# Cross-attention and experts on one core: maxima further ahead, the chain behind the row sums spread over three pairs, fewer projections among the first maxima, and the experts' high halves on ScalarE

## What is computed

```python
def xattn(x, context, Wq, Wk, Wv, Wo, bo):      # x 4x256x128 (normalized), context 4x1601x96
    q, k, v = heads(x @ Wq), heads(context @ Wk), heads(context @ Wv)
    attn = softmax(q @ k.T * 64 ** -0.5)
    return merge(attn @ v) @ Wo + bo
def ffn(h, router_w, router_b, sw1, sb1, sw2, sb2, rw1, rb1, rw2, rb2):   # 1024 tokens
    p = softmax(h @ router_w + router_b)
    weights = p where p is among the top 2 of its row, else 0
    shared = gelu(h @ sw1 + sb1) @ sw2 + sb2
    routed = sum_e weights[:, e] * (gelu(h @ rw1[e] + rb1[e]) @ rw2[e] + rb2[e])
    return shared + routed
x = x + xattn(layernorm(x), ctx)
x = x + ffn(layernorm(x))
```

## Time and profile before

| | us |
|---|---|
| median of 3 runs (lowest to highest) | 484.85 (482.22 to 485.1) |
| the profiled execution | 482.24 |
| its span, first to last instruction | 480.4 |
| PE busy / DVE / ACT / POOL in the span | 453.5 / 288.0 / 185.3 / 310.0 |
| mean share of TensorE's clock that was granted | 0.964 |

### The profile page before, as it was taken

One profiled execution on the slowest core, in us unless ns is written; L12 is line 12 of the kernel. 1 busy time (PEld: TensorE's weight loads), 2 busy tenths in 40 slices (PEclk: granted clock), 3 DMA queues, 4 the chain that ended last, 5 costly groups with the idle time before them and its releaser, 6 DMA issues.

```text
span 480.4 us, 7162 instructions
## 1 busy us (share of the span) xinstructions
PE 453.5 (94%) x2541; PEld 341.6 (71%) x2541; DVE 288.0 (60%) x569; ACT 185.3 (39%) x257; POOL 310.0 (65%) x203
## 2 busy tenths in 40 slices
PE   6989989999999899999999799999998999998896
PEld 5876757776777577767777577768776766676785
DVE  4587865665246646753466665644464437997675
ACT  4443422343544323435434232345341445454341
POOL 5939792876356937673659376745474586677682
PEclk9799998999999979999999799999997999999999
DMA  8200010000000100000002100000000000000000
GB/s 244 80 1 1 0 53 0 2 1 0 1 0 2 53 0 1 0 1 1 1 1 57 43 1 1 0 1 2 0 1 1 1 0 1 1 0 1 23 3 22
DMA packets 5194, 7.27 MB, mean 15 GB/s; under 512 B 644, under 2 KB 4136, under 8 KB 5160
## 3 DMA queue, kind: packets, MB, share of 16 engines
q1 hardware_dynamic: 5160, 6.81, 4.9%
HBM read 6.29 MB, written 0.52 MB: 14 GB/s over the span
## 4 chain that ended last, share of the span: by engine, by line
PE 86%; DVE 11%; issue 1%; ACT 1%; DVEq 0%; POOL 0%; ACTq 0%; POOLq 0%
PE ps L1076 20%; PE ps L1059 11%; PE ps L986 11%; PE ps L1060 10%; PE ps L1061 10%; PE ps L915 6%; PE ps L917 6%; PE ps L916 6%; DVE ps L807 3%; PE ps L1004 1%; PE ps L998 1%; DVE g_hi L891 1%; PE ps L992 1%; DVE probs L874 1%; DVE maxes L794 1%
## 5 line engine op out<-in xcount | busy, mean ns | idle before, releaser
L687 ACT ACTIVATE probs<-ps 128x1024 f32<-128x1024 f32 (+1 forms) x112 | 107.9, 963 | 169.0 <-PE ps L1061 167.5
L477 POOL TENSOR_TENSOR work<-work,probs 128x1024 f32<-128x1024 f32 x60 | 142.9, 2382 | 42.3 <-ACT probs L687 39.8
L794 DVE TENSOR_REDUCE maxes<-ps 128x1 f32<-128x402 f32 x256 | 135.6, 570 | 53.3 <-PE ps L986 52.5
L1076 PE MATMUL ps<-probs,v_sb 128*64 128x256 f32 (+1 forms) x832 | 96.9, 383 | 0.0
L1059 PE MATMUL ps<-g_hi,ctxT_hi 97*128 97x512 f32 (+1 forms) x208 | 86.6, 416 | 8.5 <-DVE g_hi L802 8.5
L986 PE MATMUL ps<-ctxT_hi,g_hi 96*128 96x402 f32 x256 | 82.6, 386 | 2.4 <-DVE work L810 1.1
L1060 PE MATMUL ps<-g_lo,ctxT_hi 96*128 96x512 f32 (+1 forms) x208 | 84.6, 407 | 0.0
L1061 PE MATMUL ps<-g_hi,ctxT_lo 96*128 96x512 f32 (+1 forms) x208 | 84.2, 405 | 0.0
L1076 PEld LDWEIGHTS ps<-probs,v_sb 128*64 128x64 f32 (+1 forms) x832 | 56.9, 137 | 35.8 <-issue 9.3
L475 POOL TENSOR_TENSOR work<-probs 128x1024 f32<-128x1024 f32 x15 | 35.5, 2367 | 56.8 <-issue 55.1
L986 PEld LDWEIGHTS ps<-ctxT_hi,g_hi 96*128 96x128 f32 x256 | 50.0, 203 | 22.3 <-issue 6.9
(11 more groups left out here) (137 smaller groups left out, 560.0 us busy)
## 6 DMA issues: line engine op xcount, KB each, us to landing
raw<-in_ctx_T_dram SPq DMA_DIRECT2D x3, 600.4 KB, 4.5
work<-in_L_ffn_rw_dram SPq DMA_DIRECT2D x1, 1024.0 KB, 7.4
raw<-in_ctx_T_dram SPq DMA_DIRECT2D x3, 150.8 KB, 2.5
x_sb<-in_x_dram SPq DMA_DIRECT2D x1, 384.0 KB, 5.6
early<-in_WqkT_dram SPq DMA_DIRECT2D x1, 336.0 KB, 4.9
wo_sb<-in_L_xattn_Wo_dram SPq DMA_DIRECT2D x1, 256.0 KB, 5.6
out_dram<-x_sb SPq DMA_DIRECT2D x1, 256.0 KB, 2.2
out_dram<-x_sb SPq DMA_DIRECT2D x2, 128.0 KB, 1.7
```

The source lines that it names most:

```text
L477: ops.tensor_tensor(acc, acc, pr, ALU.add).then_inc(summed, 1)
L687: nc.scalar.activation(probs[0:rows, n % SLOTS, 0:wide, :], s, ACT.Exp, scale=SCALE).then_inc(probs_ready, 1)
L794: v.tensor_reduce(maxes[:, p % 2, i * T + t, blk:blk + 1], src[:, 0:BW], AX.X, ALU.max).then_inc(ring_taken, 1)
L1076: ins = mm(o_bank[DH * i:DH * (i + 1), :], v_sb[0:rows, c, h * DH:(h + 1) * DH], probs[0:rows, n % SLOTS, j, i * S:(i + 1) * S], start=(c ...
```

## The change

It does five things. LEAD goes from 1.5 to 2.5 pairs, with the split of the next batch's context (`ctx`) moved from pair 1 to pair 0, so that maxima of the next batch can follow (`split` in `plan`). The chain behind the row sums is spread: `norm` moves from unit 2 to unit 5 of the second pair after, `xt`, `router`, `exp`, `rank` and `best` from the second to the third pair after, `wrow` to the fourth. At the start only every second maximum of (0,0) is followed by a v0, v0 uses 2 banks in place of 4, shift(0,0) comes before the last four v0 and g(0,1) behind them, the second product of the weights comes later, and 7 + 6 small matmuls whose result nobody reads stand behind the first transposes and behind g(0,0) (REST_1, REST_2). In the experts, ScalarE makes the high halves, and does so one turn later: `split` of a turn follows the Gelus and `weigh` of the next; `hid_w` has 8 slots in place of 4; `spread` follows `first`, and its ring slot is free as soon as `weigh` is done (the small memset `freed` goes). `sums` of (3,3) comes ahead of the first `split`, `exp` directly behind `router`, and `rank`, `best` of the second half ahead of the `split` and `second` of turn 7.

```diff
+REST_1 = 7
+REST_2 = 6
-LEAD = 1.5
+LEAD = 2.5
...
-            put.update({4: ("stats", 1), 8: ("stats", 2), 12: ("normal", 1)})
+            put.update({3: ("stats", 1), 6: ("stats", 2), 9: ("stats", 3)})
...
-            if n == 0 and m >= 3 and n_v0 < chunks:
+            if n == 0 and m >= 3 and m % 2:
...
-            tasks.insert(4, ("m", 1))
+            tasks.insert(8, ("m", 1))
             rest = [("v0", c) for c in range(n_v0, chunks)]
-            tasks += rest[:2] + [("shift", b, p)] + rest[2:]
+            tasks += rest[:2] + [("shift", b, p)] + rest[2:] + [("g",) + order[1]]
...
-              (2, 2): [("norm",)], (4, 2): [("ring", ("xt",))], (5, 2): [("ring", ("router",)), ("exp",)],
-              (6, 2): [("rank",), ("best",)], (3, 3): [("ring", ("wrow",))]}
+              (5, 2): [("norm",)], (2, 3): [("ring", ("xt",))], (3, 3): [("ring", ("router",)), ("exp",)],
+              (4, 3): [("rank",), ("best",)], (1, 4): [("ring", ("wrow",))]}
...
-            if p == 1 and b + 1 < batches and u < blocks:
-                main.append(("ctx", (b + 1, u)))
+            if p == 0 and b + 1 < batches and 0 < u <= blocks:
+                main.append(("ctx", (b + 1, u - 1)))
...
-                if done >= need and (at > pe or pair > n):
+                if done >= need and (at > pe or pair > n or task[0] == "max" and task[1] not in split):
...
-    amid = {2: [("ring", ("y", b))], 5: [("ring", ("xt", b))], 6: [("ring", ("router", last))]}
-    behind = {0: [("ring", ("sums",) + last_pair)], 2: [("ring", ("yt", b))], 3: [("norm", b)],
-              6: [("exp", last)], 7: [("rank", last), ("best", last)]}
+    amid = {0: [("ring", ("sums",) + last_pair)], 2: [("ring", ("y", b))], 5: [("ring", ("xt", b))],
+            6: [("ring", ("router", last)), ("exp", last)], 7: [("rank", last), ("best", last)]}
+    behind = {2: [("ring", ("yt", b))], 3: [("norm", b)]}
...
+            new = list(range(n, n + chunks))
+            out += [("first", i) for i in new]
             if e < experts:
                 out.append(("ring", ("spread", h, e)))
...
-            out += [("split", i) for i in new]
-            if h == 1 and turn == 0:
-                out.append(("ring", ("wrow", last)))
+            out += [("split", i) for i in weighted]
+            weighted = new
...
                     act.wait_ge(v0_filled, w + 1)
-                    nc.scalar.copy(v_sb[0:rows, w, :], ps[0:rows, w % 4, :]).then_inc(v0_taken, 1)
+                    nc.scalar.copy(v_sb[0:rows, w, :], ps[0:rows, w % 2, :]).then_inc(v0_taken, 1)
...
+                elif kind == "split":
...
+                    nc.scalar.copy(hid_hi[:, n % SPLITS, :], activations(n)).then_inc(hid_hi_ready, 1)
...
-                    v.tensor_copy(hid_hi[:, n % SPLITS, :], activations(n)).then_inc(hid_hi_ready, 1)
...
+                    if w == ("g", 0, 0):
+                        for _ in range(REST_2):
+                            mm(ps[0:DH, 7, 0:DH], ones[:], ones[:], start=True, stop=True)
```

More of the change, by code:

```diff
@@ L107, in plan @@
                 main += [("w2", e) for e in range(experts) if e * n_units // experts == u]
-            for ago in (1, 2, 3):
+            for ago in (1, 2, 3, 4):
                 if n < ago:
@@ L133, in plan @@
     index = {w: n for n, w in enumerate(order)}
+    split = {0}
     def ready(task):
@@ L185, in plan @@
             put(x)
+            if kind == "ctx" and w[1] == blocks - 1:
+                split.add(w[0])
         last = kind
@@ L219, in plan_experts @@
                 out += [("second", (i, part)) for i in waiting.pop(0) for part in parts[i // per]]
+            if h == 1 and turn == 0:
+                out.append(("ring", ("wrow", last)))
             if h and turn == LAG - 1:
@@ L265, in build @@
     sorts = [[w for w in ring_list if w[0] == name] for name in ("v", "back")]
-    sorts.append([w for w in ring_list if w[0] not in ("v", "back")])
+    sorts.append([w for w in ring_list if w[0] not in ("v", "back", "spread")])
     nth = {w: k for some in sorts for k, w in enumerate(some)}
@@ L433, in taken @@
                 return out_ready, nth[w] + 1
+            if w[0] == "spread":
+                return hidw_ready, weighed[items.index((w[1], w[2], HK - 1))]
             return ring_taken, nth[w] + 1
         def activations(n):
-            return (hid if items[n][1] == E else hid_w)[:, n % 4, :]
+            return hid[:, n % 4, :] if items[n][1] == E else hid_w[:, n % 8, :]
         def m_parts(i):
@@ L647, in _ @@
                 high_part(0, i)
-            act.wait_ge(s_wv, 16)
-            nc.scalar.copy(wv_hi[:], wv_sb).then_inc(wv_hi_ready, 1)
+                if i == 1:
+                    act.wait_ge(s_wv, 16)
+                    nc.scalar.copy(wv_hi[:], wv_sb).then_inc(wv_hi_ready, 1)
             for kind, w in steps:
@@ L700, in _ @@
                     ins.then_inc(lexp_ready, 1)
+                elif kind == "split":
+                    n = w
+                    if n == 0:
+                        act.wait_ge(scores_ready, LAST_UNIT)
+                    if n >= SPLITS:
+                        act.wait_ge(w2_done, n - SPLITS + 1)
+                    if items[n][1] == E:
+                        act.wait_ge(hid_ready, n + 1)
+                    else:
+                        act.wait_ge(hidw_ready, weighed[n])
+                    nc.scalar.copy(hid_hi[:, n % SPLITS, :], activations(n)).then_inc(hid_hi_ready, 1)
                 elif kind == "first":
@@ L917, in three, with keep_awake @@
                 return mm(dst, a_lo, b_hi, start=False, stop=stop)
+            def keep_awake(n):
+                for _ in range(n):
+                    mm(ps[0:DH, 4, 0:DH], ones[:], ones[:], start=True, stop=True)
             pe.wait_ge(pool_done, 1)
-            for _ in range(WARM):
-                mm(ps[0:DH, 4, 0:DH], ones[:], ones[:], start=True, stop=True)
+            keep_awake(WARM)
             def product_of_weights(i):
```

45 lines of the change are left out of this document (16 added, 29 removed).

## The result

The changed kernel takes 468.36 us (median of 4 runs, 467.81 to 470.0), the kernel before 483.63 beside it: ratio 0.969, 95% interval 0.964 to 0.974. It is faster. The profiled execution is the slowest of the four, 470.0 us, with a span of 468.2 and a granted clock of 0.984 (the other three: 0.988 to 0.991). A ratio counts only runs within 1.5% of the same kernel's quickest, and the kernel before scatters over 475.7 to 485.2 us, so further down I compare the kernels' own medians.

What follows compares the result with a forecast made beforehand. TensorE's order was taken to set the end, so gains come from its waits or clock. 482.24 - 3.8 (start) - 16.1 (shifts) + 0.6 (slots) + 3.7 (experts) = 466.6, called 467 us; range 460 to 477, own range 463 to 471.

Steps and rivals of the forecast that it cites:

- Three shifts: In (1,1), (2,1), (3,1): waits for the shift's copy go, 7.2 us, and half-clock stretches, 8.9; together 16.1 us saved.
- clock falls not tied to the waits: Rival, 17%: the three half-clock stretches come from small transposes and sums and stay; 8.9 us remain, 475.5.
- The `ctx` splits that move ... stand on engines with that same room: nothing: Context splits moved to a batch's first pair: claimed to cost nothing, since their engines have room.
- Slots: Maxima crowding into (0,2), 27 in place of 21: +0.6 us charged for waits for slots.
- The start: Up to the first scores: 29.51 becomes 25.7, 3.8 us saved, assuming the small matmuls keep the clock up.
- Experts, +3.7: Experts' part: high halves on ScalarE a turn later and weights earlier, in sum 3.7 us lost, bounds 0 and +7.
- turns 6 to 12: Experts: low halves of items 12, 13 wait behind rank and best; pause of about 4 us, +1.7 for half clock.
- steady turns: Experts: the longer chain through ScalarE's copies and the low halves adds 0.15 us a turn, +0.5 over the last turns.
- the end: Experts' end: VectorE's last two low halves stand behind GpSimd's of item 33, 7.1 us in place of 5.4, +1.7.
- the rival of slow copies: Rival, 4%: ScalarE's copies in the experts take 1.7 us each while GpSimd works, giving 494 us.
- Experts cost nothing: Rival, 15%: TensorE finds its operands in time, with no pause long enough for the clock: 463 us.
- The lead doesn't help: Rival, 9%: VectorE lags behind the plan, slots block TensorE elsewhere, half of 16.1 and 3.8 is lost: 477 us.

Runs made afterwards that it cites:

- fill_waits: Kernel before, with small matmuls in TensorE's three waits for the shift, ahead of the scores of (1,2), (2,2), (3,2): 476.69 us, ratio 0.990.
- ctx_back: Changed kernel with the ctx splits of batch 1 back in (0,1), where they stood before: 466.69 us, ratio 0.976.
- best_late: Changed kernel with rank and best of the last two batches behind the splits of turn 7 instead of ahead of them: 467.58 us, ratio 0.978.
- both_no_rest: both_moves without the 13 small matmuls of the start: 465.19 us, ratio 0.962.
- norm_early: Changed kernel with stats of batches 1 to 3 behind the start's last projection and their normal products earlier in (0,1): 471.8 us, ratio 0.986.
- all_moves: sums_late with VectorE making the low halves of the last four items instead of the last two: 458.36 us, ratio 0.948.
- both_moves: Changed kernel with batch 1's ctx splits back in (0,1) and the last batches' rank and best behind turn 7's splits: 462.26 us, ratio 0.960.
- sums_late: both_moves with the row sums of (0,0) behind the first scores of (0,2) instead of ahead of its shift: 459.42 us, ratio 0.950.

## Why the prediction was right, and where its terms were not

The time (467 against 468.4) lies in the forecast's own range of 463 to 471. But it is partly luck: two terms were off by 3.5 us and more, in opposite directions. The profiled execution, to which the terms were added up (466.6), took 470.0.

- **Three shifts, -16.1: right.** Counted from the starts of the matmuls, what the pairs (1,1), (1,2), (2,1), (2,2), (3,1) and (3,2) lose against full pace fell from 22.9 to 6.7 us, -16.2. The rival "clock falls not tied to the waits" is out for these three: the stretches went with the waits, and in fill_waits with the idle time alone.
- **"The `ctx` splits that move ... stand on engines with that same room: nothing": the step that failed.** Measured: +3.6 in (0,1), of which ctx_back gives back 3.1. Of these, 2.5 are the splits' own: best_late, with the splits as in the changed kernel but no half-clock stretch there, takes 26.89 for (0,1), ctx_back 24.38. (0,2) lost another 1.1, as its stretch was 6.83 instead of 3.41; that this comes from the splits is not shown, since best_late has them and no stretch there. I looked at who waits for GpSimd's results; what counted was who waits for its ports. The rule on shared ports (the Trainium skill, page "SBUF — State Buffer") I used only to clear ScalarE's copies, and not on the `normal` products. The change had moved these too, in a line that the diff above does not show: before, the three pairs started at 38.87, 51.03 and 56.10 and took 0.93, 0.59 and 0.59; after, at 45.62, 50.91 and 54.67, beside GpSimd's longer queue. In (1,0) and (2,0), which now hold the splits for batches 2 and 3, a projection of `v` waits for ScalarE's copy, 0.4 us each.
- **Slots, +0.6: too small.** (0,2), (0,3), (1,0) and (2,0) lose some 2 us more than before, besides the clock.
- **The start, -3.8: right in kind.** From the first maximum to the first scores before takes 20.95 and after 17.61, against the 17.1 that I summed; the clock stayed up, for which the small matmuls are the likely reason (both_no_rest). First maximum and first scores in the timeline of after, as the earlier trace rows:

```profile
9.56 1.65 PE L1000 MATMUL ps<-ctxT_hi,g_hi 96*128 96x402 f32 x4
...
27.17 0.40 PE L1077 MATMUL ps<-g_hi,ctxT_hi 97*128 97x512 f32 x1
```

  The remaining 1.0 us was lost ahead of the first maximum (9.56 instead of 8.56): the small matmuls of the warm-up (44 records) took 4.96 us instead of 4.08; the same code took 4.28 in best_late.
- **Experts, +3.7: mis-sized, measured +0.2.** Worked out from the Gelus' starts: until turn 6 -1.3 (I had -0.5); turns 6 to 12 -0.2 (I had +2.0 without that 0.5), because the stretch at half clock after the idle time (426.25) took the place of the one at 430.5 and did not come on top of it; steady turns +0.3 (+0.5); the end +1.4 (+1.7). ScalarE's copies took 0.615 us in the mean of 36 and 0.626 at most, so the rival of slow copies is out. The copies by form, first ScalarE's after, then VectorE's before: busy us, mean ns, idle ahead.

```profile
L722 ACT CAST g_hi<-probs 128x512 fp32r<-128x512 f32 x36 | 20.2, 615 | 0.0
L891 DVE CAST g_hi<-probs 128x512 fp32r<-128x512 f32 x36 | 18.6, 556 | 2.0 <-ACT probs L715 1.8
```

The 0.38 us that I took for VectorE's copy is the pace of undisturbed ones. The 36 took 0.556 in the mean, up to 1.57, so a copy on ScalarE costs 0.06 us more and not 0.24. The rule of the Trainium skill, page "Perfetto Trace Analysis", section "Optimizing Scalar/DVE Operations", would have cost up to 8.6 us by my 0.24; by the means it is 2.1. The steady turns and the end, where these copies stand in the chain, cost 1.7 together, and other stages gave it back.

"Experts cost nothing" thus had the price right, but not the reason: there was a wait of 2.80 us and a half-clock stretch behind it, and the terms cancelled. "The lead doesn't help" was wrong.

## What to carry to other kernels

Before moving work onto an engine with room, look not only at who waits for its results but at what another engine does in the gaps that the move closes: here 3.5 us of low parts in GpSimd's gaps held up VectorE's products and made (0,1) 2.5 to 3.1 us longer. When a wait ends in a half-clock stretch, the two are two gains: a few small matmuls in the wait recover the second without curing the first. And test each part of a change on its own before trusting a sum that fits.

## What the runs showed of the hardware

- VectorE's `tensor_scalar` of 128x128 between SBUF tensors: 0.33 to 0.35 us beside an idle GpSimd; up to 3.05 us in the changed kernel and 3.27 in norm_early beside GpSimd's back-to-back additions of 2.4 us. One of two columns took 2.78 us instead of 0.17. VectorE's maxima, which read PSUM, are not held up: in the changed kernel all 256 took 558 to 577 ns, beside GpSimd or not.
- Copies that round, 128x512 from SBUF to SBUF: VectorE's took 414 to 1568 ns in the kernel before, ScalarE's 602 to 626 ns in the changed one.
- The number of half-clock stretches differs from run to run of one program: the same kernel before ran at 475.7 us with clock 0.982 and at 485.0 with 0.961. The longest idle of TensorE does not settle it. Behind the start it was 1.06 us in all_moves (clock 0.999 to 1.0) and 1.08 us in both_moves (0.995), where a stretch began at 452.62, behind waits of 0.80, 0.60 and 0.18 us within 2 us. sums_late had nearly the same three waits and no stretch.
